# A fused gated cross-attention and feed-forward block: scores by four row tiles, one bank for the transposed shifts, W_proj read earlier

## The reference

```
x = x + tanh(g_xattn) * attention(layernorm(x), ctx, ctx, mask)
x = x + tanh(g_ffn)   * ffn(layernorm(x))

attention: q = query @ Wq + bq, k = key @ Wk + bk, v = value @ Wv + bv, in 16 heads of 16
           scores = q k^T / sqrt(16) + mask * -1e9;  softmax over 64 keys;  o = weights v;  o @ Wo + bo
ffn:       h = x @ quant(W_fc)^T + b_fc + 2 * (x @ A_fc^T) @ B_fc^T;  h = gelu(h)
           h @ quant(W_proj)^T + b_proj + 2 * (h @ A_proj^T) @ B_proj^T
quant(w):  round(w / s) * s with s = max|w| / 127, clipped to -128..127
```

## Time and profile before

| | us |
|---|---|
| median of three runs | 204.48 |
| lowest, highest | 203.13, 204.89 |
| the profiled execution | 204.89 |
| its span, first to last instruction | 202.9 |

### The profile page before, as it was taken

One profiled execution on the slowest core, in us unless ns is written; L12 is line 12 of the kernel. 1 busy time (PEld: TensorE's weight loads), 2 busy tenths in 40 slices (PEclk: granted clock), 3 DMA queues, 4 the chain that ended last, 5 costly groups with the idle time before them and its releaser, 6 DMA issues.

```text
span 202.9 us, 3501 instructions
## 1 busy us (share of the span) xinstructions
PE 187.9 (93%) x1241; PEld 140.4 (69%) x1241; DVE 145.4 (72%) x295; ACT 107.2 (53%) x187; POOL 108.2 (53%) x145
## 2 busy tenths in 40 slices
PE   6999965999996999999999999999998989999992
PEld 4656832566775976786778856967787748867991
DVE  2869799678289478897568979776479865954724
ACT  3151935784857446665447356643465464236521
POOL 3528979236939548539249662185377640344600
PEclk9999998799999799999999999999999999999998
DMA  6997000000060000000000000000000000010002
GB/s 182 262 251 277 22 0 2 5 0 0 2 210 0 0 0 29 0 27 29 26 0 0 3 0 26 29 26 26 0 2 5 0 29 26 0 52 3 0 0 103
DMA packets 10010, 8.38 MB, mean 41 GB/s; under 512 B 3165, under 2 KB 9722, under 8 KB 9994
## 3 DMA queue, kind: packets, MB, share of 16 engines
q1 hardware_dynamic: 9538, 8.03, 12.4%
q10 hardware_dynamic: 456, 0.14, 0.4%
...
## 4 chain that ended last, share of the span: by engine, by line
PE 72%; POOL 9%; DVE 8%; issue 6%; ACT 4%; DVEq 0%; POOLq 0%
PE ps L1190 13%; PE ps L1170 6%; PE ps L1114 6%; PE ps L1144 6%; PE ps L1103 6%; PE ps L1174 6%; POOL shifted L316 5%; PE ps L987 4%; PE ps L1124 4%; PE ps L1131 4%; PE ps L1212 2%; PE ps L1181 2%; PE ps L978 2%; PE ps L1158 2%; ACT probsT L447 2%
## 5 line engine op out<-in xcount | busy, mean ns | idle before, releaser
L316 POOL TENSOR_TENSOR shifted<-shifted,row_max 128x512 f32<-128x512 f32 x32 | 35.8, 1133 | 17.3 <-DVE row_max L752 17.2
L1190 PE MATMUL ps<-wprojT,h_hi 128*128 128x288 f32 x128 | 37.2, 314 | 1.7 <-ACT wprojT L496 1.7
L803 DVE TENSOR_TENSOR h_lo<-wfc_sb,h_hi 128x512 fp32r<-128x512 f32 x32 | 25.3, 797 | 17.4 <-POOL h_hi L335 17.4
L1190 PE MATMUL ps<-wprojT,h_lo 128*128 128x288 f32 x128 | 35.6, 301 | 0.0
L335 POOL TENSOR_SCALAR h_hi<-wfc_sb 128x512 fp32r<-128x512 f32 x32 | 21.9, 689 | 23.9 <-ACT wfc_sb L632 23.9
L632 ACT ACTIVATE wfc_sb<-ps,bias_cols,wscale 128x512 f32<-128x512 f32 x32 | 24.5, 779 | 18.8 <-PE ps L1181 16.9
L1190 PEld LDWEIGHTS ps<-wprojT,h_hi 128*128 128x128 f32 x128 | 24.9, 195 | 2.8 <-ACT wprojT L496 2.2
L447 ACT ACTIVATE probsT<-ps 128x512 f32<-128x512 f32 x32 | 19.0, 598 | 14.2 <-PE ps L1114 13.9
L739 DVE TENSOR_TENSOR shifted<-ps,mask_neg 128x512 f32<-128x512 f32 x32 | 20.8, 683 | 7.4 <-PE ps L1103 7.2
L1190 PEld LDWEIGHTS ps<-wprojT,h_lo 128*128 128x128 f32 x128 | 24.8, 194 | 0.2
L1114 PE MATMUL ps<-ident,shifted 128*128 128x128 f32 x128 | 20.2, 284 | 4.2 <-POOL shifted L316 4.2
...
## 6 DMA issues: line engine op xcount, KB each, us to landing
...
```

The costliest lines, as they stand in the source:

```text
L316: nc.gpsimd.tensor_tensor(shifted[:, slot], shifted[:, slot], row_max[:, slot].unsqueeze(2).broadcast_to([P, HH, KC]), ALU.subtract)\
L803: nc.vector.tensor_tensor(h_lo[:, f], hidden[:, f % HIDDEN_SLOTS], h_hi[:, f].bitcast(F32), ALU.subtract).then_inc(h_split, 1)
L1190: last = nc.tensor.matmul(dst[:, 0:DOWN], h[:, f, t * P:(t + 1) * P], wprojT[:, f], start=(f == 0 and n == 0), stop=(f == FC - 1 and n == ...
```

## The change

Four things are done.

1. Scores use four row tiles of 32 rows (2 heads) with 128 columns of k each, into banks 0 to 3, so a call has 32 matmuls in place of 16. `k_hi` and `k_lo` are two heads wide, by a new `pair_rows`. DVE masks a unit out of all four banks in one operation.
2. All transposed shifts go through bank 4. den and o of the first half share bank 5, those of the second take banks 2 and 3. `up` slice 6 moves from bank 2 to 6, the two wprojT from 6 and 3 to 0 and 1, kT 1 from 3 to 4.
3. The order: scores(c+1, 0) is after f = 7 in place of f = 3, scores(c+1, 1) after the first half `down` of the next attention. DVE and POOL do the first pair's mask, maxima and shifts after all their slices. In chunk 0 the denominators are ahead of transpose 4 and the weighted values behind transpose 6; in chunks 1 to 3 the weighted values are behind transpose 7.
4. W_proj is transposed after f = 4 and 5 and read behind gelus 4 and 5.

The diff, with most of its unchanged lines left out:

```diff
--- before.py
+++ after.py
@@ -21,22 +21,20 @@
-SCORED = (3, 7)
-UP_BANKS = (6, 5, 2, 3, 7, 4, 2, 5)
+UP_BANKS = (6, 5, 2, 3, 7, 4, 6, 5)
 def bank_sequence(chunks):
-             (("first_q", 1), 7), (("kT", 1), 3), (("q", 0, 1), 5), ("v", 4), ("aT", 6), ("bprojT", 7), (("bfcT", 0), 5),
+             (("first_q", 1), 7), (("kT", 1), 4), (("q", 0, 1), 5), ("v", 4), ("aT", 6), ("bprojT", 7), (("bfcT", 0), 5),
     for c in range(chunks):
-        order += [(("scores", c, p, h), h) for p in range(4) for h in range(2)]
-        order += [(("shiftT", c, u), 2 + u % 2) for u in range(8)]
-        for m in range(2):
-            order += [(("den", c, m), 4), (("o", c, m), 5)]
+        order += [(("scores", c, p, i), i) for p in range(4) for i in range(4)]
+        order += [(("shiftT", c, u), 4) for u in range(8)]
+        order += [(("den", c, 0), 5), (("o", c, 0), 5), (("den", c, 1), 2), (("o", c, 1), 3)]
@@ -48,7 +46,7 @@
-            order += [(("wprojT", 0), 6), (("wprojT", 1), 3)]
+            order += [(("wprojT", 0), 0), (("wprojT", 1), 1)]
@@ -93,7 +91,7 @@
-        quad_rows = sb("quad_rows", [P, 4])
+        quad_rows, pair_rows = sb("quad_rows", [P, 4]), sb("pair_rows", [P, 2])
@@ -110,7 +108,7 @@
-        k_hi, k_lo = (sb(n, [P, NB, KD, 4, KC], F32R) for n in ("k_hi", "k_lo"))
+        k_hi, k_lo = (sb(n, [P, NB, KD, 2, KC], F32R) for n in ("k_hi", "k_lo"))
@@ -270,7 +268,9 @@
-                .then_inc(consts_ready, 1)
+                .then_inc(idents_zeroed, 1)
+            pool.wait_ge(idents_zeroed, 4)
+            nc.gpsimd.tensor_tensor(pair_rows[:], quad_rows[:, 0:2], quad_rows[:, 2:4], ALU.add).then_inc(consts_ready, 1)
             def inverse_deviation(n, tiles, count):
@@ -291,8 +291,8 @@
             def keys_low(e, blocks):
-                nc.gpsimd.tensor_tensor(k_lo[:, e, blocks], kT_lo[:, blocks, e].unsqueeze(2).broadcast_to([P, size, 4, KC]),
-                                        quad_rows[:].unsqueeze(1).unsqueeze(3).broadcast_to([P, size, 4, KC]),
+                nc.gpsimd.tensor_tensor(k_lo[:, e, blocks], kT_lo[:, blocks, e].unsqueeze(2).broadcast_to([P, size, 2, KC]),
+                                        pair_rows[:].unsqueeze(1).unsqueeze(3).broadcast_to([P, size, 2, KC]),
             def lora_parts():
@@ -384,8 +384,9 @@
-                    if c < LAST and f in (4, 6):
-                        shift(c + 1, f // 2 - 2)
+                if c < LAST:
+                    shift(c + 1, 0)
+                    shift(c + 1, 1)
         def _(act):
@@ -633,10 +634,8 @@
-                    if c == 0 and f == 6:
-                        read_wprojT(0)
-                if c == 0:
-                    read_wprojT(1)
+                    if c == 0 and f in (4, 5):
+                        read_wprojT(f - 4)
@@ -694,8 +693,8 @@
             def keys_high(e, blocks):
-                                        kT_hi[:, blocks, e].bitcast(F32).unsqueeze(2).broadcast_to([P, size, 4, KC]),
-                                        quad_rows[:].unsqueeze(1).unsqueeze(3).broadcast_to([P, size, 4, KC]),
+                                        kT_hi[:, blocks, e].bitcast(F32).unsqueeze(2).broadcast_to([P, size, 2, KC]),
+                                        pair_rows[:].unsqueeze(1).unsqueeze(3).broadcast_to([P, size, 2, KC]),
             def largest_weights(n):
@@ -728,28 +727,25 @@
-            def mask_half(c, p, h):
-                first = 2 * p % SHIFT_SLOTS
-                key = ("scores", c, p, h)
-                wait_full(dve, key)
-                if c:
-                    for u in (2 * p, 2 * p + 1):
+            def mask_pair(c, p):
+                for i in range(4):
+                    wait_full(dve, ("scores", c, p, i))
+                for u in (2 * p, 2 * p + 1):
+                    if c:
-                row = c % C * T + 2 * p % T
-                nc.vector.tensor_tensor(shifted[:, first:first + 2, 4 * h:4 * h + 4],
-                                        bank(key).rearrange("p (j i k) -> p j i k", j=2, i=4),
-                                        mask_neg[:, row:row + 2].unsqueeze(2).broadcast_to([P, 2, 4, KC]), ALU.add)\
-                    .then_inc(freed(key), 1)
-
-            def mask_pair(c, p):
-                for h in range(2):
-                    mask_half(c, p, h)
+                    j = u % 2
+                    last = nc.vector.tensor_tensor(shifted[:, u].rearrange("p (b i) k -> p b i k", b=4),
+                                                   ps[:, 0:4, j * P:(j + 1) * P].rearrange("p b (i k) -> p b i k", i=2),
+                                                   mask_neg[:, c % C * T + u % T].unsqueeze(1).unsqueeze(1)
+                                                   .broadcast_to([P, 4, 2, KC]), ALU.add)
+                last.then_inc(freed(("scores", c, p, 0)), 1)
+                wait_read(dve, ("scores", c, p, 0))
+                for i in range(1, 4):
+                    dve.sem_inc(freed(("scores", c, p, i)), 1)
             def row_maxima(c, u):
-                slot = u % SHIFT_SLOTS
-                for h in range(2):
-                    wait_read(dve, ("scores", c, u // 2, h))
-                nc.vector.tensor_reduce(row_max[:, slot], shifted[:, slot], AX_X, ALU.max).then_inc(max_ready, 1)
+                wait_read(dve, ("scores", c, u // 2, 0))
+                nc.vector.tensor_reduce(row_max[:, u], shifted[:, u], AX_X, ALU.max).then_inc(max_ready, 1)
             def normalise(c, m, parts=1):
@@ -936,10 +932,10 @@
-                    if c < LAST and f in (1, 2):
-                        mask_half(c + 1, 0, f - 1)
-                    if c < LAST and f in (3, 4):
-                        row_maxima(c + 1, f - 3)
+                if c < LAST:
+                    mask_pair(c + 1, 0)
+                    row_maxima(c + 1, 0)
+                    row_maxima(c + 1, 1)
             for c in range(CHUNKS):
@@ -1094,17 +1090,17 @@
-                dst = [claim(("scores", c, p, h)) for h in range(2)]
+                dst = [claim(("scores", c, p, i)) for i in range(4)]
-                        for h in range(2):
-                            rows = slice(h * HP, (h + 1) * HP)
-                            last = nc.tensor.matmul(dst[h][:, j * 256:(j + 1) * 256], q[rows, m, t * P:(t + 1) * P],
+                        for i in range(4):
+                            rows = slice(32 * i, 32 * i + 32)
+                            last = nc.tensor.matmul(dst[i][:, j * P:(j + 1) * P], q[rows, m, t * P:(t + 1) * P],
-                                done(last, ("scores", c, p, h))
+                                done(last, ("scores", c, p, i))
             def transpose_shifted(c, u):
@@ -1242,12 +1238,10 @@
                     up_high(c, f)
                     up_low(c, f)
                     up_lora(c, f - EARLY)
-                    if c == 0 and f == 5:
-                        transpose_wproj(0)
-                    if c < LAST and f in SCORED:
-                        scores(c + 1, SCORED.index(f))
-                    if c == 0 and f == 7:
-                        transpose_wproj(1)
+                    if c == 0 and f in (4, 5):
+                        transpose_wproj(f - 4)
+                    if c < LAST and f == 7:
+                        scores(c + 1, 0)
                 for f in range(FC - EARLY, FC):
                     up_lora(c, f)
 
@@ -1268,13 +1262,13 @@
                 transpose_shifted(0, 3)
                 spread_wmax(0)
                 scores(0, 3)
-                transpose_shifted(0, 4)
                 pe.wait_ge(pair_ones_ready, 1)
                 denominators(0, 0)
+                transpose_shifted(0, 4)
                 transpose_shifted(0, 5)
+                transpose_shifted(0, 6)
                 pe.wait_ge(v_blocks_ready, 2 * NB)
                 weighted_values(0, 0)
-                transpose_shifted(0, 6)
                 transpose_shifted(0, 7)
                 denominators(0, 1)
                 weighted_values(0, 1)
@@ -1294,6 +1288,7 @@
                     wait_read(pe, ("wprojT", 0))
                     pe.wait_ge(aT_ready, 1)
                 down(c - 1, 0, 0)
+                scores(c, 1)
                 transpose_shifted(c, 0)
                 down(c - 1, 1, 0)
                 transpose_shifted(c, 1)
@@ -1309,13 +1304,13 @@
                 transpose_shifted(c, 4)
                 denominators(c, 0)
                 transpose_shifted(c, 5)
-                weighted_values(c, 0)
                 if c == 1:
                     wait_read(pe, "bprojT")
                 finish_down(c - 1, 0)
                 transpose_shifted(c, 6)
                 turn_t2(c - 1, 1)
                 transpose_shifted(c, 7)
+                weighted_values(c, 0)
 
             def attention_body(c):
                 attention_start(c)
```

## The result

The changed kernel takes 230.98 us (median of 5 runs, 227.84 to 234.12) against 204.48 before: ratio 1.1225, 95% interval 1.1141 to 1.1309. This ratio is that of the faster executions (227.84, 228.19, 230.98), with the two slowest left out. The direction was forecast, the size was not: 219.0 with a range up to 227. The profiled execution took 230.98 us for a span of 229.1.

A forecast was written before the change was run, and what follows sets the result against it. TensorE was taken as the bound, busy 93% and dense, so gaps in its order add to the end. Terms of 12.85 us plus 1.6 for the clock made 14.5: 219.4 from the profiled 204.89, 219.0 beside the median; range 210 to 227.

The forecast's parts named there:

- Part 1: Scores by four row tiles: weight loads set the pace, a quad takes 0.117 us like a pair; 0 us.
- Part 2: Attentions of chunks 1 to 3: transposed shifts in one bank wait for each exponential; +2.6, +2.6, +1.7 us.
- Part 3: Attention heads of chunks 1 to 3: moved first scores start the mask and shift chain later; +0.15, +1.0, +1.0 us.
- Part 4: W_proj reads before chunk 1's first scores: a wait of 2.5 us replaces 3.35 us of wait and slow clock.
- Part 5: Chunk 0's attention: transposed shifts wait for v's reads and the exponentials; +2.5 us, bounds +1 and +3.5.
- Part 6: Last down: waits for bank 6, which the last gelu now holds; +1.3 us in full.
- Part 7: Clock: new gaps cost one more half-clock stretch on dense work, between none and three; +1.6 us.
- The rival at 229: Scores: loads or instructions cannot follow four row tiles; +10 us, so 229; chance 0.10.
- rival "faster": Scores' quads run at streaming pace, -7.5 us, with only a third of the gaps, 4.3; 201.5 us; chance 0.07.

The follow-up runs named there:

- a2: c1_fill with scores again as pairs of 64 rows and 256 columns in the same four banks; 220.3 us, ratio 1.0868.
- s1: The kernel before with all transposed shifts in bank 2, nothing else; 211.84 us, ratio 1.0451.
- b1: The changed kernel with transposed shifts of chunks 1 to 3 alternating in banks 4 and 5, den in 2, o in 3; 227.24 us, ratio 1.1135.
- o1: The kernel before with only the first scores, their masks, maxima and shifts moved as in the change; old banks and pairs; 205.21 us, ratio 1.0144.
- c5: c1_fill with the second wprojT behind the first scores, in bank 7, read behind gelu 7, and fewer fillers; 218.25 us, ratio 1.0726.
- c1_fill: The changed kernel with unused small bf16 matmuls put into TensorE's gaps in chunk 0 and the attention starts; 219.28 us, ratio 1.084.
- c4: c1_fill with v in bank 7 instead of 4 and without the 20 fillers ahead of the first transposed shift; 220.29 us, ratio 1.0813.
- c3: c1_fill with the last down's column tiles in banks 0, 6, 1, 2 instead of 6, 0, 1, 2; 217.95 us, ratio 1.0726.
- a1: The changed kernel with scores again as pairs of 64 rows and 256 columns in the same four banks; 228.35 us, ratio 1.127.
- a4: The changed kernel with scores as pairs of 64 rows again, repeated beside a3_changed; 228.61 us, ratio 1.1261.
- q2: The kernel before with 72 unused full matmuls, then 64 unused quads, between last up and last down; 224.62 us, one execution.
- q3: The kernel before with 64 unused quads, then 72 unused full matmuls, between last up and last down; 231.31 us, one execution.
- a3_changed: The changed kernel measured once more, unaltered; 227.41 us, ratio 1.1198.
- c2: The changed kernel with fillers only in the three gaps at the head of each attention start; 227.99 us, ratio 1.1251.

## Why the prediction was wrong

The direction and the places of the gaps were right; the clock's term was mis-sized, and it is most of the miss. By the profiles the change is 26.2 us where 14.5 was forecast. The clock's net part is 10.5 instead of 1.6, the other terms are 15.7 instead of 12.85.

- **Part 1 (quads, 0):** right in time. 0.11 us a quad, at half clock 0.213 for 32 to 256 columns; undone alone (a2) it is 1.3 us by the spans. The Trainium skill (TensorEngine Tiling, Theoretical Speedup) gives up to four times for 32 rows and up to two for 64; with four new weight loads of 128 columns a step the runs show no such difference.
- **Part 2 (+2.6, +2.6, +1.7):** right, slightly low. At full clock +3.0, +3.0, +1.9: T to T is 1.41 to 1.44 instead of 1.34. In s1 the bank alone accounts for 1.8 of each, in b1 for 1.4; that the moved W(0) is the rest is by difference, not tested alone.
- **Part 3 (+0.15, +1.0, +1.0):** +0.8 and +0.8 at full clock in chunks 2 and 3 (o1 has the same 0.8 for chunk 3 by the order alone), +0.6 in chunk 1.
- **Part 4 (a wait of 2.5 for 3.35):** the wait is there with 2.35, ahead of S0, for the second read of W_proj (c5). What it sets off was not counted: see below.
- **Part 5 (+2.5, bounds +1 and +3.5):** too small. The +2.6 between the profile before and c1_fill agrees by luck, since the first has a half-clock stretch worth 1.6 in chunk 0 and the second none; at full clock in both it is +4.2, outside the bounds. T0 behind v is 0.7 of it (c4), the one bank some 1.8 (s1, a stretch of 3.41 us on both sides); the rest, some 1.7, was not taken apart.
- **Part 6 (+1.3):** +1.3, and c3 takes it away.
- **Part 7 (clock, +1.6, "between none and three" stretches): this step failed.** I took the old stretch of 3.4 us as the size of one, and one more of them. The profile shows 37.6 us at half instead of 6.8 (both without the last few us), worth 12.1 us against c1_fill, or 10.5 net of the stretch that chunk 0 had before (the old one in chunk 1 is in part 4). What the term missed is how long the clock stays down. It took the length from a stretch with full matmuls behind its wait; behind the new gaps of chunks 1 and 2 stand quads, and there it stayed down for 10.24 to 17.07 us (3.41 once, in b1's chunk 2), where with pairs in the same places it was 3.41 or nothing (a1 and a4), and in the bench 3.41 behind full matmuls and 17.07 behind quads (q2, q3). The long stretch at 35.5 in chunk 0 is not explained by this: it has no quads in it, only transposes, D, W and waits, and in a3_changed it is 3.41.
- **The rival at 229** (loads or instructions can't follow four tiles) came nearest by its number. Its mechanism did not happen: the quads step 0.11.
- The 201.5 of the rival "faster" adds up to 201.7; nothing rests on it.

The Trainium skill (TensorE: Matmul & The Clock Gate, Terms) puts the penalty at half of the time spent at half clock. By that 37.6 us would be 18.8; the runs show 12.1, a third. One reason is that PE waits for part of a stretch anyway (8.19 of 10.2 us busy in the one of chunk 0 at 35.5). In the bench, where PE never waits, 13.66 us more at half (17.07 less 3.41) cost 6.4, near the rule's 6.8.

The clock also accounts for most of the spread between executions of the changed kernel. Twelve of them (five of the result, seven of a3_changed) have spans of 224.2 to 232.2 us and mean clocks of 0.954 to 0.904; twice the clock's missing share times the span gives 20.6 to 44.6 us at half. Above c1_fill's 217.0 that is 7.2 us for 20.6 at half, 12.1 for 37.6 and 15.2 for 44.6: a third each time.

Left open: why the same gap brings the clock down in one execution and not in another. The wait of 2.35 us ahead of chunk 1's first scores was followed by half clock in the profiles of the changed kernel, a3, b1, a1 and a4, and not in c2; the wait for W_proj was followed by it in the kernel before (1.75 us) and not in o1 (1.90).
